# Attention scores in fp32, four heads at a time in four groups of 32 rows and four banks

## The reference, cut to what matters

```
q = (x @ wq).reshape(B, T, H, D)        # B 16, T 512, H 16 heads, D 16
lat = x @ w_down
k = (lat @ wk_up).reshape(B, T, H, D)
v = (lat @ wv_up).reshape(B, T, H, D)
q, k = _apply_rope(q, cos, sin), _apply_rope(k, cos, sin)
scores = jnp.einsum('bqhd,bkhd->bhqk', q, k) * scale
pages = jnp.arange(T) // 64
scores = jnp.where(pages[None, :] <= pages[:, None], scores, min)
attn = jax.nn.softmax(scores, axis=-1)
out = jnp.einsum('bhqk,bkhd->bqhd', attn, v).reshape(B, T, E) @ wo
```

## Time and profile before

| | |
|---|---|
| Median of 3 runs (lowest to highest) | 2078.34 us (2069.44 to 2090.56) |
| The profiled execution's own time | 2082.85 us |
| Its span, first to last instruction | 2081.1 us |
| First score matmul to last probability | about 609 to 1414 us |
| TensorE busy | 1787.1 us, 86% |
| VectorE, ScalarE, GpSimd busy | 60%, 51%, 42% |
| Mean granted TensorE clock | 0.951 of 2.4 GHz |

### The profile page before, as it was taken

One profiled execution on the slowest core, in us unless ns is written; L12 is line 12 of the kernel. 1 busy time (PEld: TensorE's weight loads), 2 busy tenths in 40 slices (PEclk: granted clock), 3 DMA queues, 4 the chain that ended last, 5 costly groups with the idle time before them and its releaser, 6 DMA issues. The chain is left out here.

```text
span 2081.1 us, 33794 instructions
## 1 busy us (share of the span) xinstructions
PE 1787.1 (86%) x11330; PEld 1141.7 (55%) x11330; DVE 1253.2 (60%) x3079; ACT 1071.1 (51%) x2132; POOL 871.6 (42%) x938
## 2 busy tenths in 40 slices
PE   5999997999737899999999999996999999866773
PEld 3656655888622344445545444553556656755672
DVE  4878885443345677777777777761878877322221
ACT  4766763111024577777777777773667765100000
POOL 1101101688736566666666665500101100555553
PEclk9999998999967899999999999997999999999986
DMA  2443533999734333434444444312233431777763
GB/s 82 129 129 128 161 130 107 254 260 260 154 102 122 112 113 114 113 113 113 121 125 130 131 119 113 95 41 83 79 92 105 130 114 53 202 189 183 179 164 40
DMA packets 218233, 269.71 MB, mean 130 GB/s; under 512 B 18378, under 2 KB 185322, under 8 KB 218094
## 3 DMA queue, kind: packets, MB, share of 16 engines
q1 hardware_dynamic: 193518, 230.20, 36.6%
q0 software_dynamic: 24576, 37.77, 9.8%
HBM read 136.17 MB, written 80.25 MB: 104 GB/s over the span
## 5 line engine op out<-in xcount | busy, mean ns | idle before, releaser
L1259 DVE TENSOR_REDUCE a_smax<-a_p_ring 128x1 f32<-128x512 f32 (+2 forms) x768 | 353.8, 505 | 153.6 <-PE a_p_ring L1346 148.5
L1161 ACT ACTIVATE a_probs<-a_p_ring 128x512 f32<-128x512 f32 x640 | 363.8, 606 | 104.1 <-PE a_p_ring L1358 102.4
L1346 PE MATMUL a_p_ring<-p_ks,p_qs 100*128 100x512 bf16 (+3 forms) x1024 | 247.4, 306 | 45.9 <-ACT a_probs L1161 20.6
L611 ACT ACTIVATE e_silu<-e_p_up 88x256 f32<-88x256 f32 x128 | 48.6, 380 | 458.7 <-PE e_p_up L653 360.8
L653 PE MATMUL e_p_up<-e_xT,h_w 128*88 128x128 f32 x2048 | 259.1, 282 | 0.0
L47 POOL TENSOR_TENSOR f_rstd<-f_mv,eps 128x4 f32<-128x4 f32 x32 | 25.6, 799 | 554.2 <-DVE f_mv L41 549.6
L1358 PE MATMUL a_p_ring<-p_qs,p_ks 103*128 103x512 bf16 (+3 forms) x1024 | 244.2, 305 | 7.0 <-ACT a_probs L1161 6.7
L653 PEld LDWEIGHTS e_p_up<-e_xT,h_w 128*88 128x88 f32 x2048 | 243.3, 164 | 0.2
L455 PE MATMUL f_p_up<-f_xnT,f_ws1T 128*128 128x512 f32 x384 | 187.7, 612 | 1.5 <-ACT f_xnT L250 1.5
L575 POOL DMA_INDIRECT e_got<-rows,slot_token x128 | 126.5, 988 | 145.0 <-issue 135.3
L625 DVE TENSOR_TENSOR e_hidden<-e_silu,e_p_up 88x256 f32<-88x256 f32 x128 | 53.4, 417 | 221.5 <-ACT e_silu L611 165.3
(11 more groups left out here) (142 smaller groups left out, 3243.4 us busy)
## 6 DMA issues: line engine op xcount, KB each, us to landing
h_w<-w_in SPq DMA_DIRECT2D x128, 352.0 KB
p_qs<-a_parts SPq DMA_DIRECT2D x192, 128.0 KB, 2.5
p_ks<-a_parts SPq DMA_DIRECT2D x192, 128.0 KB, 2.5
h_w<-w_in SPq DMA_DIRECT2D x128, 176.0 KB
rows<-f_row SPq DMA_DIRECT2D x32, 640.0 KB, 6.9
h_x<-x_in SPq DMA_DIRECT2D x16, 512.0 KB, 5.9
acc<-h_x SPq DMA_DIRECT2D x16, 512.0 KB, 2.8
acc<-blank SPq DMA_DIRECT2D x16, 512.0 KB, 4.0
```

The costliest lines, as they stand in the source:

```text
L1161: nc.scalar.activation(to[:], p_score[s][:], ACT.Exp, scale=SCALE).then_inc(score_free[s], 1)
L1259: ins = nc.vector.tensor_reduce(smax[:, t, 4 * g + h:4 * g + h + 1], p_score[s][:, at:at + length], AX.X, ALU.max)
L1346: ins = nc.tensor.matmul(p_score[s][:, at:at + length], qs[1 - u][0:SR + MASK, 4 * g + h, t * P:(t + 1) * P], ks[1 - u][0:SR + MASK, 4 * g ...
```

## The change

Queries and keys stay in fp32 and are no longer split. Four heads lie in the four groups of 32 partitions: 16 rows of the head, four of mask, and one for the maximum. `qs` and `ks` have three buffers instead of two. The matmuls of four heads for the same piece are issued one after the other, each in its own row group and to its own bank, and an S step now takes four banks of the ring at once: `take_scores` waits for all four before the first matmul. C of two quads (q 0 and 1) shares the four banks, so a turn still uses 40 banks for S1 and 40 for S2, in ten steps of each kind. Stacking takes 16 transfers a batch instead of 24. HIGH, SPLIT and NEG are gone. The maxima are turned by an fp32 matmul against the identity and go down in one transfer; a row of -1 beside the keys subtracts them. `probs` has twelve buffers instead of ten, the weights' columns are ordered otherwise on the host, and the places in the lists are new. `experts` no longer waits for a mask made by DVE; 24 transfers place the masks.

```diff
-Q_SLOTS = [HIGH, HIGH, MIDDLE, HIGH, LOW, MIDDLE]
-K_SLOTS = [HIGH, MIDDLE, HIGH, LOW, HIGH, MIDDLE]
-SR = HD * len(Q_SLOTS)
...
+GROUP = 4
+QUADS = H // GROUP
+HP = 32
 MASK = 4
-TOP = 3
-QUADS = H // 4
-HP = 32
+ROWS = HD + MASK
...
-    return [(2 * n, 1, 0, 256), (2 * n + 1, 1, 256, 256)]
...
+        return [(0, 2, 0, 384), (0, 0, 384, 128)]
+    return [(0, 1, 0, 256), (1, 1, 256, 256)]
...
+MAXIMA_ORDER = [("A", 0), ("B", 0), ("A", 1), ("B", 1), ("C", 0)]
...
+def probs_of(e, entering=False):
+
+    steps = [("S2", e, "A", 0)]
+    if entering:
+        steps += [("PV", e - 1, "B", 1)]
+    steps += [("S2", e, "C", 0), ("PV", e, "A", 0)]
+    if entering:
+        steps += [("OUT", 2 * e - 1)]
+    return steps + [("S2", e, "B", 0), ("PV", e, "C", 0), ("S2", e, "A", 1), ("PV", e, "B", 0), ("S2", e, "B", 1),
+                    ("PV", e, "A", 1), ("PV", e, "C", 1), ("OUT", 2 * e)]
...
-    pre.qs = [sb(f"qs{u}", [P, H, T], BF16) for u in range(2)]
-    pre.ks = [sb(f"ks{u}", [P, H, T], BF16) for u in range(2)]
+    pre.qs = [sb(f"qs{u}", [P, QUADS, T]) for u in range(BUFFERS)]
+    pre.ks = [sb(f"ks{u}", [P, QUADS, T]) for u in range(BUFFERS)]
...
-                def stack(half, j, u):
-                    heads = slice(half * H // 2, (half + 1) * H // 2)
-                    for r, to, slots in ((Q_TILES[half], qs, Q_SLOTS), (K_TILES[half], ks, K_SLOTS)):
-                        sp.wait_ge(low_ready, 4 * j + r + 1)
-                        for s, part in enumerate(slots):
-                            sp.dma_start(to[u][s:SR:len(slots), heads, :],
-                                         parts[r][:, part, :]).then_inc(stack_loaded[half], 16)
...
+                def stack(r, j):
+
+                    e, to = r // 2, (qs if r in Q_TILES else ks)[j % BUFFERS]
+                    if (j - BUFFERS, e) in last_scores:
+                        bank, used = last_scores[j - BUFFERS, e]
+                        sp.wait_ge(score_ready[bank], used + 1)
+                    sp.wait_ge(rope_ready, 4 * j + r + 1)
+                    for h in range(GROUP):
+                        sp.dma_start(to[group_rows(h, 0, HD), 2 * e:2 * e + 2, :],
+                                     qk[r][group_rows(h, 0, HP), :]).then_inc(stack_loaded[e], 16)
...
-                            for part in range(TOP):
-                                row, heads = SR + MASK + part, slice(e * H // 2, (e + 1) * H // 2)
-                                sp.dma_start(qs[parity][row:row + 1, heads, :],
-                                             smaxT[e][part * H // 2:(part + 1) * H // 2, :]
-                                             ).then_inc(smax_loaded[e], 16)
+                            sp.dma_start(qs[of % BUFFERS][ROWS:P:HP, 2 * e:2 * e + 2, :],
+                                         smaxT[e][:]).then_inc(smax_loaded[e], 16)
...
-                        elif step[0] == "HIGH":
-                            r = step[1]
-                            pool.wait_ge(high_ready, 4 * j + r + 1)
-                            if j == 0:
-                                pool.wait_ge(rest_ready, 2)
-                            nc.gpsimd.tensor_tensor(qk[r][:], qk[r][:], parts[r][:, HIGH, :],
-                                                    ALU.subtract).then_inc(rest_ready, 1)
-                        elif step[0] == "SPLIT":
-                            r = step[1]
-                            pool.wait_ge(middle_ready, 4 * j + r + 1)
-                            if j == 0:
-                                pool.wait_ge(low_ready, 2)
-                            nc.gpsimd.tensor_tensor(parts[r][:, LOW, :], qk[r][:], parts[r][:, MIDDLE, :],
-                                                    ALU.subtract).then_inc(low_ready, 1)
...
+                            for h, (s, used) in enumerate(take_banks(scores)):
+                                act.wait_ge(score_ready[s], used + 1)
+                                nc.scalar.activation(probs[probs_at(step[2]) + h][:], p_score[s][:], ACT.Exp,
+                                                     scale=SCALE).then_inc(score_free[s], 1)
...
-                        if kind == "HIGH":
-                            r = step[1]
-                            wait_count(act, stack_loaded[r // 2], 192 * j)
-                            act.wait_ge(rope_ready, 4 * j + r + 1)
-                            nc.scalar.copy(parts[r][:, HIGH, :], qk[r][:]).then_inc(high_ready, 1)
-                        elif kind == "SPLIT":
-                            r = step[1]
-                            act.wait_ge(rest_ready, 4 * j + r + 1)
-                            nc.scalar.copy(parts[r][:, MIDDLE, :], qk[r][:]).then_inc(middle_ready, 1)
...
-                    def take_score():
-                        s, used = scores.next()
-                        wait_count(pe, score_free[s], used)
-                        return s
-
+                    def take_scores():
+                        banks = take_banks(scores)
+                        for s, used in banks:
+                            wait_count(pe, score_free[s], used)
+                        return banks
...
-                            s = take_score()
-                            for h, t, at, length in score_pieces(group, k):
-                                ins = nc.tensor.matmul(p_score[s][:, at:at + length],
-                                                       qs[1 - u][0:SR + MASK, 4 * g + h, t * P:(t + 1) * P],
-                                                       ks[1 - u][0:SR + MASK, 4 * g + h, 0:length],
-                                                       start=True, stop=True)
-                            ins.then_inc(score_ready[s], 1)
+                            _, e, group, second = step
+                            if step == maxima_of(e)[0]:
+                                pe.wait_ge(stack_loaded[e], 2 * GROUP * 16 * (n + 1))
+                                if n == 0 and e == 0:
+                                    pe.wait_ge(pre.mask_placed, 16 * 2 * GROUP * BUFFERS)
+                            banks = take_scores()
+                            queries, keys = qs[n % BUFFERS], ks[n % BUFFERS]
+                            for q, t, at, length in score_pieces(group):
+                                for h, (s, used) in enumerate(banks):
+                                    rows, quad = group_rows(h, 0, ROWS), 2 * e + second + q
+                                    ins = nc.tensor.matmul(p_score[s][:, at:at + length],
+                                                           queries[rows, quad, t * P:(t + 1) * P],
+                                                           keys[rows, quad, 0:length], start=True, stop=True)
+                                    if at + length == T:
+                                        ins.then_inc(score_ready[s], 1)
+                            maxima_read[e] = score_free[s], used + 1
...
+                                for h, (s, used) in enumerate(banks):
+                                    rows, quad = group_rows(h, 0, ROWS + 1), 2 * e + second + q
+                                    ins = nc.tensor.matmul(p_score[s][:, at:at + length],
+                                                           keys[rows, quad, t * P:(t + 1) * P],
+                                                           queries[rows, quad, t * P:T], start=True, stop=True)
+                                    if at + length == T:
+                                        ins.then_inc(score_ready[s], 1)
+                            freed[e, group, second] = s, used + 1
...
-                                ins = nc.tensor.transpose(p_misc[m][:, t * P // 2:(t + 1) * P // 2].bitcast(BF16),
-                                                          smax_parts[e][:, t, :], ident16[:])
+                                ins = nc.tensor.matmul(p_misc[m][0:H // 2, t * P:(t + 1) * P],
+                                                       smax[:, t, e * H // 2:(e + 1) * H // 2], w.ident[:],
+                                                       start=True, stop=True)
...
+    mask[MASK, T:] = -1
```

More of the change, by code:

```diff
@@ L818, in with_stack @@
[L818 to L827 removed]
+    from_to(0.0, 0.36, of_batch(-1, maxima_of(0))) + from_to(0.36, 0.72, of_batch(-1, maxima_of(1)))
```

339 lines of the change are left out of this document (116 added, 223 removed).

## The result

The changed kernel takes **2526.0 us** (median of four runs, 2518.8 to 2530.7) against 2079.9 us of the kernel before in the same session: 1.216 times the time, with a 95% interval of 1.212 to 1.219. The sign of the forecast and its waits for banks held, the size did not: 2365 us was forecast, with 2480 as the range's upper end. The profiled execution took 2525.25 us.

The account below looks back on a forecast made before the run. PE was taken as the bound. Fourteen turns at 19.2 us of added waiting and work (269), entry -5, masks +1, start +5, last turn +2 gave 2350 us; about 1 us a turn for the clock made 2365, range 2240 to 2480.

Parts of the forecast that it names:

- The sign of the forecast: Whole kernel: the change makes it slower, chance 0.93, against 0.04 for the same and 0.03 for faster.
- The bound, and what comes off ACT, POOL and DMA: Full turn: PE bounds, busy 46.1 of 48.8 us; work taken off ACT, POOL and DMA gains nothing.
- The ring: Score banks in a turn: PE waits 21 us instead of 2.8 for four banks at once; turn 68 us, 19.2 more.
- The step of four banks: Score matmuls on PE: 0.95 us per four-bank step, twenty steps 19 us, a turn's work 47.4 us.
- The clock: Full turns: waits bring a stretch at 1.2 GHz, about 1 us a turn, moving 2350 to 2365 us.
- Rival 1: Attention turns: clock falls often, mean near 0.85, some 8 us more a turn, about 2465 us; chance 0.14.
- my own list: PE's bank waits followed through one changed turn, among them 1.95 us twice, 2.0, 2.3 and 1.9.
- Rivals 2 to 4: Row groups serial (0.07) or no overlap (0.03), about 2510 or 3150; ring costs half, 2225 (0.08); faster, 2047 us (0.03).
- The entry: Attention's beginning: fewer stack transfers let the first score start at about 604.5 instead of 609.3, -5 us; masks +1.
- The start and the end: Before the first full turn: +5 us (between -15 and +20); last turn, S2 alone: +2 us.

Follow-up runs that it names:

- e12: The changed kernel with score matmuls on all 32 rows of each group (128 in all, added rows mostly zeros), waits kept: 2368.2 us, 1.135 times the kernel before.
- e1: The changed kernel with five overwritten bf16 filler matmuls on 128 rows at the eleven longest-waiting steps a turn: 2392.0 us, 1.149 times the kernel before.
- e14: The kernel before with its bf16 score matmuls on only 20 rows instead of 100 and 103, order and banks kept: 2283.4 us, 1.094 times the kernel before.
- e7: The changed kernel with shortened DVE maxima reads and ACT exponentials reading 128 columns, most results left out: 2196.3 us, 1.055 times the kernel before.

## Why the prediction was wrong, step by step

**The bound, and what comes off ACT, POOL and DMA: right.** Their work went and nothing followed from it. No wait in the turns ends on a stack transfer.

**The ring: right in place, near in size.** The forecast was a turn of 68 us; it is 67.97 in e12 and 68.28 in e1, with nearly full clock. That it fits so closely is luck: two errors cancel in it. In the profile's terms e12 idles 15.06 us a turn; each of its twelve waits begins about 0.20 us later than in mine, since it starts at the end of a record of 1.15 us and not 0.95 us after the step's start. So in my terms it is about 17.5 us, where I had 21, and the longest is 1.7 + 0.2 and not 2.3. Work is then 50.5 us and not 47.4.

**The step of four banks: too cheap.** 1.08 us at 2.4 GHz against my 0.95. Twenty steps make 2.6 of the 3.1 us by which the work exceeds my 47.4. (My sum also put at nothing the 1.5 us between its own 19 us for twenty steps and the 17.5 us of before; some smaller saving that I did not trace must stand against it.) PV's column groups gave 1.00 us and the wider weights 0.08 more, together just the 1.08; I then took 0.13 off for neighbours in the same mode, and nothing bears that out. The Trainium skill (TensorE: Matmul & The Clock Gate, section Part 3: Packing small matmuls) gave 3.07 times, hence an estimated 1.12 us; the measured 3.44/1.08 = 3.2 times agrees with it better than my 3.6.

**The clock: the step that failed.** I put "about 1 us a turn for a stretch at 1.2 GHz" into the sum. Measured, the change's turn is 78.14 us and e12's 67.97 with the same waits: 10.2 us a turn. Over twelve turns that is 122 us, and 158 over the kernel (2526.0 less 2368.2), most of the rest in the attention's start and end. Without it the forecast is near: e12 takes 2368 us, where my sum had 2350 without a term for the clock and 2365 with it.

**Rival 1 named the symptom and missed the cause.** It had the clock near 0.85 (measured 0.82) and 112 us for it, and 0.14 as its chance. But I drew it from the length of waits and from PE's busy share in the earlier trace rows, where the products have 128 or 88 rows, and I read even these badly. I wrote that no wait there exceeded 1.78 us; two longer ones lie in the very window with clock 0.83:

```profile
1939.54 0.44 PE L645 MATMUL e_p_turn<-ident,e_got 128*128 128x128 f32 x2 [2.58 <-DMA e_got<-rows,slot_token]
1949.62 0.44 PE L645 MATMUL e_p_turn<-ident,e_got 128*128 128x128 f32 x2 [2.46 <-DMA e_got<-rows,slot_token]
```

The longest wait in the window with clock 1.00 is 1.7 us, as long as e12's longest. And five waits of my own list exceed 1.78 us, not two. By my reading of waits alone e12, which waits as long as the change, should have fallen as far, and it stayed at 0.98; e14, which hardly waits, should have stayed up, and it fell to 0.81. What I left out is that the change brings PE's score streams from 100 and 103 rows to 80 and 84 while making room for waits. The rows are in the earlier trace rows and in the diff. In the changed kernel it takes both: narrow streams with short waits held 1.00 (e7, longest 0.8 us), full rows with long waits 0.98 (e12), narrow streams with long waits got 0.82 (the change).

The Trainium skill (TensorE: Matmul & The Clock Gate, section A second HAM failure mode: psum-queue depth-cycling) says that short idle gaps between groups of matmuls, as banks are cycled through, make the clock swing between its levels. Here that is half of it: with such gaps, up to 1.7 us, and 128 rows e12 keeps 0.98.

**Rivals 2 to 4: wrong.** Row groups load and stream together, as the records above show. The waits were not halved, nor absent.

**The entry: too cheap.** I had the first score matmul 4 us earlier; it comes 1.6 us later:

```profile
602.02 2.62 SPq L950 DMA_DIRECT2D p_qs<-a_qk  x4
...
606.73 2.46 SPq L950 DMA_DIRECT2D p_ks<-a_qk  x4
...
610.88 2.08 PE L1220 MATMUL a_p_ring<-p_ks,p_qs 20*128 20x512 f32 x8 [5.16 <-DMA p_ks<-a_qk]
```

The wait for the stacks is halved as forecast (5.16 us against 11.11), but the attention begins some 6 us later, and this part is not explained.

**The start and the end: near, but for the clock.** The output projections at which I cut lie some 0.44 of the way into a turn (`TAIL` places the first there). So the stretch from the first score matmul to the first full turn's projections holds 0.44 of a turn's growth, and my forecast for it is 5 + 0.44 x 19.2 = 13 us. e12 has 16 (149.5 against 133.7) and the change 28. Behind the thirteenth projections 1.56 turns and the last one are left: 1.56 x 19.2 + 2 = 32 us by my forecast, 34 in e12 and 52 in the change.

## What to carry to other kernels

Count how many rows of the array each product uses before you make it "cheaper". Here a bf16 product of 20 rows took as long as one of 100 (0.38 to 0.39 us for 384 and 128 columns at 2.4 GHz, in e14 and in the earlier trace rows), the narrow ones cost every product of the turn its clock, and padding with zero rows cost no time. Pipeline by bank, not by step: if one product fills several banks and they become readable together, PE pays its readers' latency at every step that shares banks with the one before it. (Whether a ring that holds two whole steps removes this was not tested; five banks instead of six made it worse.) Price a new wait and a changed clock from the turn as a whole, and take the clock as a term of its own with its own evidence, not as a rounding of the waits.

## What was unexpected in the hardware

- **Active rows and the granted clock.** The score matmuls of the kernel before on 20 rows and not 100: mean clock 1.00 to 0.81, at 0.51 us of idle time a turn. The change on 128 rows and not 80: 0.82 to 0.98, with waits unchanged. The change with one wait for each bank, likewise: 0.85 to 1.00. Fillers of 128 rows: 1.00 and 0.99; of 20 rows: 0.83 and 0.86. In e12 44 of the added rows hold zeros, so for those it was enough that they are addressed.
- **Four row groups in fp32.** 512 columns of four heads take 1.08 us at 2.4 GHz, in eight records or in sixteen, and eight loads of 20 x 128 weights overlap with one another.
- **What stays open.** How rows, columns and waits combine into the level that is granted was not measured beyond these pairs. e7 has 80 and 84 rows and short waits, e14 fewer rows and nearly no waits; no kernel here has 20 rows and long waits, or 100 rows and waits of 1.7 us in the attention. Full rows are no guarantee either: the waits of 2.46 and 2.58 us in the expert stage, between products of 128 and 88 rows, go with a clock of 0.83.
